# Two-term reciprocal broadcast and four instead of three attention steps per prologue chunk in a two-layer transformer kernel

## The reference

```python
xn = _layernorm(x, axis=-1)
x = x + _L0_attn_ref(xn, Wq, bq, Wk, bk) + _L0_ffn_ref(xn, Wr, W1, W2)
xn = _layernorm(x, axis=-1)
x = x + _L1_attn_ref(xn, Wq1, Wk1, Wv1, Wo1) + _L1_ffn_ref(xn, weight, alpha, bias)
# in both attentions
attn = jax.nn.softmax(attn, axis=-1)
out = jnp.einsum('bhnm,bhmd->bhnd', attn, v)
```

## Time and profile before

| What | Value |
|---|---|
| runs, in us | 6900.99, 6924.92, 7552.33 |
| their median | 6924.92 |
| the profiled execution, time | 6905.96 |
| its span, slowest core (core 1) | 6904.4 |
| spans of the 8 cores | 6848.8 to 6904.4 |
| TensorE busy in the span | 5265.0 (76%) |
| ScalarE busy | 1925.1 (28%) |
| VectorE busy | 1352.3 (20%) |
| GpSimd busy | 1060.1 (15%) |
| granted clock, mean of core 1 | 0.885 |

### The profile page before, as it was taken

The page is one execution under the profiler, slowest core; times in us unless marked ns, Lnnn a source line. Parts: engine busy times, 40 slices in busy tenths (PEclk is TensorE's granted clock), DMA queues, the critical chain, the costliest instruction groups (busy, mean ns, idle before and its releaser), DMA issues.

```text
span 6904.4 us, 82752 instructions; the slowest of 8 cores (6848.8 to 6904.4 us)
## 1 busy us (share of the span) xinstructions
PE 5265.0 (76%) x23175; PEld 2131.1 (31%) x23175; DVE 1352.3 (20%) x2532; ACT 1925.1 (28%) x2813; POOL 1060.1 (15%) x1169
## 2 busy tenths in 40 slices
PE   3666666637989999999999999999999534555536
PEld 0222222213434434434434444444444111111102
DVE  5111122121010010100101010101010543333326
ACT  0355555541111111111111111121212024555530
POOL 0233333332222222222222200000000000000000
PEclk9888887778999999999999999999999666777768
DMA  1534434346777777777777644443434100000011
GB/s 61 162 118 138 126 113 145 109 162 193 228 239 218 229 241 219 219 251 228 219 243 232 225 167 151 156 151 147 147 147 148 36 13 13 4 7 3 4 55 68
DMA packets 205103, 989.67 MB, mean 143 GB/s; under 512 B 23014, under 2 KB 33518, under 8 KB 137082
## 3 DMA queue, kind: packets, MB, share of 16 engines
q1 hardware_dynamic: 92922, 573.29, 24.2%
q0 software_dynamic: 111744, 411.09, 19.9%
HBM read 841.69 MB, written 142.61 MB: 143 GB/s over the span
## 4 chain that ended last, share of the span: by engine, by line
PE 60%; DMA 13%; ACT 11%; DVE 9%; issue 6%; DVEq 0%; ACTq 0%; SPq 0%; POOL 0%; POOLq 0%
PE bankA L742 22%; PE bankA L763 21%; ACT exp L360 7%; DMA w2buf<-sw 6%; DMA w1buf<-sw 5%; PE bankB L350 5%; PE bankA L338 2%; PE bank L488 2%; ACT rtmpB L914 1%; PE bankA L1114 1%; PE bankA L1215 1%; DVE rb L455 1%; DVE rb L1065 1%; DVE xnTs L292 1%; DVE t1s L289 1%
## 5 line engine op out<-in xcount | busy, mean ns | idle before, releaser
L763 PE MATMUL bankA<-hid,w2buf 128*128 128x512 bf16 x8192 | 1794.2, 381 | 116.9 <-DMA w2buf<-sw 88.0
L742 PE MATMUL bankA<-xnTs,w1buf 128*128 128x512 bf16 x8192 | 1800.6, 381 | 68.2 <-DMA w1buf<-sw 68.1
L750 ACT ACTIVATE hid<-bankA 128x512 bf16<-128x512 f32 x1024 | 611.6, 597 | 3148.4 <-PE bankA L742 3148.4
L763 PEld LDWEIGHTS bankA<-hid,w2buf 128*128 128x128 bf16 x8192 | 797.2, 98 | 1113.9 <-issue 177.0
L742 PEld LDWEIGHTS bankA<-xnTs,w1buf 128*128 128x128 bf16 x8192 | 798.5, 98 | 1079.6 <-issue 146.7
L360 ACT ACTIVATE exp<-bankA,colpool 128x1024 bf16<-128x1024 f32 x832 | 906.8, 1114 | 428.5 <-PE bankA L338 392.1
L771 DVE TENSOR_TENSOR mtmp<-bankA,cbs 128x512 f32<-128x512 f32 x256 | 177.1, 692 | 3401.4 <-PE bankA L763 3401.4
L711 POOL CAST castb<-stg 128x1024 bf16<-128x1024 f32 x256 | 271.1, 1059 | 1478.0 <-DMA stg<-l0w 1478.0
L694 POOL CAST castb<-stg 128x2048 bf16<-128x2048 f32 x128 | 243.4, 1901 | 1042.5 <-DMA stg<-l0w 1042.5
L110 POOL DMA_DIRECT2D stg<-l0w x384 | 331.9, 864 | 220.5 <-DVE wkbf L310 202.4
L350 PE MATMUL bankB<-exp,vG 128*65 128x512 bf16 x640 | 256.0, 463 | 132.9 <-DVE exp L371 75.8
(11 more groups left out here) (212 smaller groups left out, 3071.2 us busy)
## 6 DMA issues: line engine op xcount, KB each, us to landing
w1buf<-sw SPq DMA_DIRECT2D x256, 1024.0 KB, 6.9
w2buf<-sw SPq DMA_DIRECT2D x256, 1024.0 KB, 7.0
stg<-l0w POOLq DMA_DIRECT2D x128, 1024.0 KB, 7.6
stg<-l0w POOLq DMA_DIRECT2D x256, 512.0 KB, 6.1
sw<-castb POOLq DMA_DIRECT2D x128, 512.0 KB, 3.3
sw<-castb POOLq DMA_DIRECT2D x256, 256.0 KB, 3.7
xTs<-xT SPq DMA_DIRECT2D x8, 1024.0 KB, 17.1
wtf<-l1wt SPq DMA_DIRECT2D x16, 512.0 KB
```

Source lines behind the costliest of these rows:

```text
L742: e.matmul(bnk[:, :], w1buf[:, slot * 4096 + dc * NT + fp * 128: slot * 4096 + dc * NT + (fp + 1) * 128], xnch(dc)[:, t0:t0 + NT], start=( ...
L750: pb.op("scalar", lambda e, f=f, bnk=bnk: e.activation(hid[:, f * NT:(f + 1) * NT], bnk[:, :], AF.Relu), reads=[bkkey], writes=[f"hid{f % ...
L763: e.matmul(bnk[:, :], w2buf[:, slot * 4096 + fc * 128:slot * 4096 + (fc + 1) * 128], hid[:, fc * NT:(fc + 1) * NT], start=(fc == 0), stop= ...
```

## The change

The closings of both attention stages broadcast the reciprocal as the sum of two bf16 rows: the cast row `hi` and the rest, `lo = rr - hi`. This takes one more VectorE operation and one more matmul, which adds to the same bank; the copy to SBUF now waits for the second matmul. And in attention 0 each prologue chunk is followed by four calls of the generator instead of three.

```diff
                     pb.op("vector", lambda e: e.tensor_copy(hi, rr),
                           reads=[f"rrow{h12}"], writes=[f"rhi{h12}"])
+                    pb.op("vector", lambda e: e.tensor_tensor(lo, rr, hi, ALU.subtract),
+                          reads=[f"rrow{h12}", f"rhi{h12}"], writes=[f"rlo{h12}"])
                     pb.op("tensor", lambda e: e.matmul(
-                        bank[bb][:, :], onesb[0:1, 0:128], hi, start=True, stop=True),
-                        reads=[f"rhi{h12}", "onesb"], writes=[f"b{bb}"],
+                        bank[bb][:, :], onesb[0:1, 0:128], hi, start=True, stop=False),
+                        reads=[f"rhi{h12}", "onesb"],
                         wait=pb._dep_waits((), [f"b{bb}"]))
+                    pb.op("tensor", lambda e: e.matmul(
+                        bank[bb][:, :], onesb[0:1, 0:128], lo, start=False, stop=True),
+                        reads=[f"rlo{h12}", "onesb"], writes=[f"b{bb}"])
                     rbs = rb2[:, h12 * NT:(h12 + 1) * NT]
...
                     if gen is not None:
-                        for _ in range(3):
+                        for _ in range(4):
                             next(gen, None)
```

## The result

The changed kernel's runs take 7012.5 to 7033.6 us; the ratio to those of the kernel before is 1.0135, with a 95% interval of 1.0093 to 1.0176. On the 6906.0 us of the profiled execution the ratio makes +93 us (+64 to +122). The forecast was 7023 us, +117, which is above this but still inside the interval. The profiled execution after takes 7012.5 us, 106.5 more than the one before.

The account below looks back on a forecast made before the run. Chains of waits, not a saturated engine, were taken to bound the attention stages. 101 + 8 + 16 - 8 = +117 us on 6906.0 gave 7023 us (+1.7%), range 6965 to 7075.

Parts of the forecast that it names:

- What bounds the kernel: Attention stretches: no engine saturated, chains of waits set the time, namely the flush and the plain step's loop.
- Part 1: Closings in both attention stages: subtraction and second matmul add 0.79 us to each of 128, +101 us, +8 beside GpSimd.
- rival A: Closings: the subtraction is short, 426 ns, so 32 us less, 6991 us; chance 10%.
- Part 2: Attention 0, heads 1 to 7: four steps behind each chunk instead of three, 2.2 us a head, +16 us.
- the block: Six ktm chunks behind a head's final flush, ahead of the norms: 7.1 us where 4.5 before, +2.5 us a head.
- Given back: Expert stage: GpSimd converts more weights during the longer first stage (75 us), which saves 8 us there.
- What a run can tell: Whole kernel: a measurement can tell about 2% from no change, or 138 us (7044 us).
- B: Behind flushes: the longer flush holds the clock down for more steps, +45 us, 7068 us; chance 12%.
- C: Attention 0: not slower, the fourth step fills ScalarE's gaps, together 133 us, 6874 us; chance 3%.
- D: Closings: second matmul might lengthen nothing, hidden behind ScalarE, leaving +8 us, 6914 us; chance 2%.

Follow-up runs that it names:

- e4: Changed kernel with three generator calls, subtraction kept but its result not broadcast (one matmul); ratio 0.9995 to the kernel before.
- e3: Changed kernel with three generator calls, subtraction left out, second matmul reading a row of zeros set once per stage; one run, 6965.0 us.
- e2: Kernel before with four generator calls per chunk instead of three, no second term; ratio 1.0019 to the kernel before.
- e1: Changed kernel with three generator calls again, subtraction and second matmul kept; 7007.7 and 7044.0 us, ratio 1.0128 to the kernel before.
- e5: As e1, but the subtraction made twice in a row; 7098.8 and 7107.6 us, quotient of means to the kernel before 1.027.
- e7: As e1, but the two heads' closings of a flush side by side in stages; one run 6923.0 us, timed again ratio 0.9986 to before.
- e8: Kernel before (three calls, one term) with the two heads' closings side by side; 6838.6 and 6841.9 us, timed again ratio 0.9908 to before.

## Why the prediction was right or wrong

**What bounds the kernel: right.** The flush is a chain in series that ends on TensorE, in both stages. e4 and e3 show it from two sides: the subtraction is free beside the chain, and the matmul in it is not.

**Part 1: right in size.** 0.79 us a closing was forecast; the timeline shows 0.79 and attention 1 gives 51.1 / 64 = 0.80. The subtraction takes 680 ns (0.68 forecast); with one f32 input it is as long as with f32 alone, and rival A falls. Beside GpSimd it is 0.10 longer on the slowest core and 0.07 by the median of the cores (0.12 to 0.13 forecast), so the +8 us for this were some 5.

**Part 2: right in size, by terms that were each a little off.** Forecast: +2.5 us for the block and -0.3 for the rest. A pair got 2.4 (e2) to 2.9 us longer (168.3 and 168.7 against e1's 165.8). The block costs 8.2 - 5.0 = 3.2 us, for a ktm chunk takes 1.18 us at the low clock and not 1.08: my 0.11 for the bias matmul was too short (0.21 to 0.22 from its start at 906.00 to the next chunk). The rest gave back some 0.8 more than it took, where 0.3 was forecast; that the two errors cancel is luck. The granted clock is 0.50 throughout the six chunks (905 to 912 us of the slowest core).

**Given back: wrong in size.** This is the step of the prediction that failed, and it makes the forecast too high: 8 us forecast, 25 found by the medians of the cores (21 in the expert stage, 4 ahead of it) and 18 by the means (14 and 4), over two profiles of each kernel. The attention terms came out within 1 us together, so this term accounts for the difference between +117 and the +103 (medians) or +108 (means) of the profiles.

Part of the term was right. GpSimd makes 0.12 casts a us ahead of the experts and 0.09 beside them, and its last cast comes 2411 to 2414 us behind the first expert block before and 2303 to 2318 after, so about 100 us less of the stage are spent beside it (75 x 0.350/0.273 = 96 forecast). An expert block takes 122.6 and 123.1 us beside GpSimd before and 112.8 without it, so 0.08 us are lost in each us of company. That makes 8 us, as forecast.

What the term lacked is the rest. The stretch between attention 0 and the experts was put at nothing; it gets shorter by 0.04 us for each us that attention 0 is longer (a line through the twelve profiles of the table, scatter 1 us), 3 us for 77. In the expert stage the same line falls by 0.20 us per us by medians (0.16 by means) with 6 us of scatter round it, 12 to 15 us for 77; my rate was 8/75 = 0.11. The loss per us of company is a little lower in the changed kernels (0.075 and 0.079 against 0.079 and 0.084), and this makes up the rest of the 21 us arithmetically. But it is within what two profiles of one kernel scatter, so why the expert stage gave back more than 8 us, and how much of it is scatter, stays open. No run was made that changes GpSimd's work alone.

The marks of the stage on the slowest cores (first and last start) were, before and after:

```profile
L727 DVE COPY cbs<-bankB x32: 677/684/692, 1587.1 to 5286.1; 128x512 f32<-128x512 f32 x32
```

```profile
L732 DVE COPY cbs<-bankB x32: 676/684/692, 1643.9 to 5338.1; 128x512 f32<-128x512 f32 x32
```

3699.0 and 3694.2 us: a single core of each shows next to nothing of it, which is why all eight cores are used. The first and last starts of GpSimd's later casts on the same cores, before and after:

```profile
L711 POOL CAST castb<-stg x256: 1040/1040/1584, 370.5 to 4003.8; 128x1024 bf16<-128x1024 f32 x128
```

```profile
L716 POOL CAST castb<-stg x256: 1040/1040/2208, 368.7 to 3983.1; 128x1024 bf16<-128x1024 f32 x128
```

GpSimd ends 21 us earlier in the changed kernel although the experts begin 57 us later.

**What a run can tell: wrong.** The prediction took 2% (138 us) as the least that a measurement of this kernel tells from no change. The interval here is 0.8% wide and lies wholly above 1, so a slowdown of 1.35% is told clearly. Two slips in its figures changed nothing: 4.56 matmuls a us are 9% above 4.18, and 8% is how far 4.18 lies below 4.56, which is what the sum uses; and A with part 2 at its lowest gives 6991 - 16 - 15 = 6960, not 6965.

**The rivals.** A falls by the duration of the subtraction. B falls by e5 in attention 1: twice the wait, twice the cost. C falls by e2, whose pairs got longer and not shorter; in the changed kernel a projection chunk with four steps takes 6.85 us, where 6.80 was forecast without any gap filled. D falls with e1, whose attention stages are 104 us longer than before. The sum with the measured give-back in place of mine would have been 101 + 8 + 16 - 25 = +100 us (+107 with the 18 of the means), where the stage marks show +103 (+108).

## What to carry to other kernels

An added operation costs what it adds to the chain that is waited for: the same subtraction was free beside a matmul, and in front of a second one the two together cost 0.79 us. When such a chain has two alike parts behind each other on in-order engines, write them in stages side by side; here that took back 130 us of attention by the stage marks (e1 against e7), more than the 104 that the second term had cost there, and left 57 us of its price (e7 against e8). And when a stage ahead gets longer, work of another engine that runs on beside it moves out of the next stage, so part of the loss comes back there (here 18 to 25 us of 124).

## What the runs showed of the hardware

A tensor_tensor with one f32 and one bf16 input and bf16 output takes 680 ns for 1x512 (679 for 1x512 and 693 for 128x512 with f32 alone, 426 for 128x512 all in bf16). Beside GpSimd's casts the same subtraction takes 784 ns on average on the slowest core and 2366 at most. An operation with a single input in SBUF meets GpSimd too: the cast of the row takes 412 ns on average in attention 1 and 532 in attention 0, where GpSimd casts (medians of the cores, before), and up to 2106 on the slowest core:

```profile
L448 DVE CAST rhl<-rrow x64: 406/415/2106, 292.2 to 1485.5; 1x512 bf16<-1x512 f32 x64
```

The granted clock fell to 0.50, the 1.2 GHz level, at the flushes as before (795 to 800 us after, 614 to 619 before). In attention 1, 1.6 or 3.2 us of longer idle time on TensorE in each flush cost their own length.
